# Graph-network kernel on one core: the layers of a tile one step closer to its edge sums, x loaded two steps ahead, the low parts of all tile sums on VectorE

## What is computed

```
h    = max(layernorm(x), 0)                              # 12500 x 128, eps 1e-5
agg  = segment_sum(edge_attr_48, dst, 12500)             # 12500 x 48
u    = graph_globals[0]                                  # one row for all nodes
out  = x + relu(concat(h, agg, u) @ W1 + b1) @ W2 + b2   # hidden width 256
```

## Time and profile before

| | us |
|---|---|
| median of 3 runs | 279.07 (278.94 to 281.57) |
| the profiled execution | 280.1 |
| its span, first to last instruction | 278.1 |
| TensorE busy in the span | 249.7 |
| VectorE busy | 218.8 |
| ScalarE busy | 145.0 |
| GpSimd busy | 103.1 |

### The profile page before, as it was taken

How to read it: one execution, slowest core, us unless ns; L and a number is a source line. 1 busy time by engine, 2 the same in 40 slices (tenths; PEclk the granted TensorE clock), 3 DMA queues, 4 the chain that set the end, 5 groups by cost and what they waited for, 6 DMA issues and landing times.

```text
span 278.1 us, 17414 instructions
## 1 busy us (share of the span) xinstructions
PE 249.7 (90%) x7448; PEld 200.0 (72%) x7448; DVE 218.8 (79%) x557; ACT 145.0 (52%) x315; POOL 103.1 (37%) x111
## 2 busy tenths in 40 slices
PE   7756468999999999989989989999899999999893
PEld 2646456887788779769768867877787787687572
DVE  1797737889988888968978888889789879885394
ACT  2555482564455556536544735654464455357640
POOL 9192103325532551451353245235415523532210
PEclk9977958999999999999999999999999999999998
DMA  7999958899999999999999999999999999999611
GB/s 250 368 364 341 336 182 273 271 387 365 388 384 384 386 378 388 366 380 345 379 359 370 388 380 338 390 379 386 380 366 382 378 357 387 369 333 380 257 40 57
DMA packets 70874, 94.50 MB, mean 340 GB/s; under 512 B 4324, under 2 KB 64260, under 8 KB 70854
## 3 DMA queue, kind: packets, MB, share of 16 engines
q1 hardware_dynamic: 69802, 94.29, 96.5%
q10 hardware_dynamic: 956, 0.00, 0.2%
q0 software_dynamic: 96, 0.00, 0.0%
HBM read 87.88 MB, written 6.40 MB: 339 GB/s over the span
## 4 chain that ended last, share of the span: by engine, by line
PE 62%; DMA 23%; DVE 7%; issue 3%; ACT 2%; POOL 1%; SPq 1%; DVEq 0%; POOLq 0%
PE group_bank L1051 22%; DMA edge_buf<-in_edge_attr 20%; PE hidden_bank L1098 12%; PE out_bank L1116 11%; PE window_bank L1073 6%; PE hidden_bank L1102 3%; PE hidden_bank L1104 3%; DMA x_buf<-in_x 3%; PE out_bank L1088 3%; DVE onehot L804 2%; PE window_bank L1138 2%; DVE rel_rows L759 2%; PE hidden_bank L1036 1%; ACT normed_x L601 1%; ACT rel L574 1%
## 5 line engine op out<-in xcount | busy, mean ns | idle before, releaser
L804 DVE TENSOR_TENSOR onehot<-rel,const_bank 128x896 f32<-128x896 f32 (+1 forms) x122 | 125.4, 1030 | 29.7 <-PE group_bank L1051 22.1
L1051 PE MATMUL group_bank<-edge_buf,onehot 128*32 128x48 f32 x6454 | 89.1, 211 | 6.4 <-DMA edge_buf<-in_edge_attr 3.6
L1051 PEld LDWEIGHTS group_bank<-edge_buf,onehot 128*32 128x32 f32 x6454 | 80.6, 113 | 15.5 <-DVE onehot L804 7.4
L535 POOL TENSOR_TENSOR tile_sums<-agg,tile_sums 48x512 fp32r<-48x512 f32 x22 | 28.1, 1277 | 133.1 <-ACT tile_sums L623 133.1
L1098 PE MATMUL hidden_bank<-normed_t,w_node 128*128 128x512 f32 (+1 forms) x100 | 52.7, 608 | 1.1 <-issue 1.0
L1116 PE MATMUL out_bank<-w_sb,hidden 128*128 128x128 f32 x384 | 47.7, 278 | 1.4 <-ACT normed_t L612 1.4
L1116 PEld LDWEIGHTS out_bank<-w_sb,hidden 128*128 128x128 f32 x384 | 44.7, 192 | 1.6 <-issue 1.6
L601 ACT ACTIVATE normed_x<-x_buf,shift,inverse 128x128 f32<-128x128 f32 x98 | 40.2, 482 | 1.9 <-DVE shift L864 1.9
L633 ACT ACTIVATE hidden<-hidden_bank,hidden_bias 128x512 f32<-128x512 f32 (+1 forms) x50 | 33.5, 671 | 13.3 <-PE hidden_bank L1104 13.3
L1102 PE MATMUL hidden_bank<-tile_sums,w_high 112*128 112x512 f32 (+1 forms) x50 | 39.3, 787 | 0.0
L586 ACT ACTIVATE sums_high<-group_bank 128x96 fp32r<-128x96 f32 (+1 forms) x49 | 13.2, 269 | 46.3 <-PE group_bank L1051 46.3
(11 more groups left out here) (93 smaller groups left out, 214.8 us busy)
## 6 DMA issues: line engine op xcount, KB each, us to landing
edge_buf<-in_edge_attr SPq DMA_DIRECT2D x97, 672.0 KB, 7.4
edge_buf<-in_edge_attr SPq DMA_DIRECT2D x24, 504.0 KB, 7.9
x_buf<-in_x SPq DMA_DIRECT2D x24, 256.0 KB, 8.6
out<-out_buf SPq DMA_DIRECT2D x23, 256.0 KB, 6.6
dst_rows<-in_dst SPq DMA_DIRECT2D x3, 448.5 KB, 8.7
dst_rows<-in_dst SPq DMA_DIRECT2D x1, 252.3 KB
out<-out_buf SPq DMA_DIRECT2D x1, 224.0 KB
edge_buf<-in_edge_attr SPq DMA_DIRECT2D x1, 168.0 KB, 6.7
```

The lines of the kernel that those rows point to most:

```text
L535: pool.tensor_tensor(sums_tile(k, STACK_LOW), agg_tile(k), sums_tile(k, 0).bitcast(fp32), ALU.subtract)\
L804: dve.tensor_tensor(onehot[:, c0:c0 + cols, :], rel[:, r0:r0 + cols].unsqueeze(2).to_broadcast([P, cols, WINDOW]), ramp_const.unsqueeze(1) ...
L1051: done = pe.matmul(group_bank[h][WINDOW * j:WINDOW * (j + 1), n * F_EDGE:(n + 1) * F_EDGE], onehot[:, (g0 + j) * EDGES_PER_ROW + r, :], ed ...
```

## The change

It reorders all five engines' lists.
- Layers: first_layer of tile s - 1 (not s - 2) runs in step s, after sums of part 1 and turn_x of tile s; second_layer of tile s - 2 follows the sums of part 0. Node matmuls of both halves come first, then the wait for tile_low.
- x of tile s + 2 is loaded in step s, after both parts of the edges; its moments are taken a step earlier.
- tile_low of every tile is VectorE's; GpSimd keeps x_plus_b2 and add_out. window_base is loaded at two places of a step, once each.
- dst blocks 1 to 3 are turned in steps 2 to 4. keep_clock runs 8 and 4 times, not 14 and 8. One of two GpSimd zeroings of agg goes ahead of places().
- In the tail the last tile of x is turned into `group_bank[1]`.

```diff
--- before.py
+++ after.py
@@ sync @@
-                if s < tiles - 1:
-                    load_x(last_tile() if s + 1 == tiles - 1 else At(s + 1))
+                    load_part(At(s + 1), 1)
+                if s + 2 < tiles:
+                    load_x(last_tile() if s + 2 == tiles - 1 else At(s + 2))
+                if s == 1:
+                    load_dst(3)
...
-                if s + 1 < steps:
-                    load_part(At(s + 1), 1)
@@ gpsimd @@
             for s in range(steps):
-                if 2 <= s < full_steps:
-                    pool.wait_ge(xb_ready, s)
-                    tile_low(At(s - 2))
-                    pool.wait_ge(tile_low_ready, s + 1)
-                if s >= 3:
-                    add_out(At(s - 3))
                 x_plus_b2(last_tile() if s == tiles - 1 else At(s))
-            add_out(At(tiles - 3))
+                if s >= 2:
+                    add_out(At(s - 2))
@@ scalar @@
+            for s in range(1, full_steps):
+                following = last_tile() if s + 1 == tiles - 1 else At(s + 1)
                 copy_sums(At(s), 0)
+                if s == 1:
+                    bias()
+                if s >= 2:
+                    copy_out(At(s - 2))
+                if 2 <= s <= blocks:
+                    copy_rel(s - 1)
+                tile_high(At(s - 1))
                 copy_sums(At(s), 1)
+                deviate(following)
+                relu_hidden(At(s - 1))
+                copy_turned(At(s))
+                normalise(following)
+                if s < blocks:
+                    relative(s)
@@ vector @@
             for s in range(1, full_steps):
                 n = At(s + 1)
+                add_window(At(s - 1), 1, base[1])
+                make_placing(At(s), 1)
...
                 make_onehot(n, 0)
+                base[0] = window_base(At(s), 0)
                 make_onehot(n, 1)
+                low_sums(At(s), 0)
                 make_onehot(n, 2)
+                add_window(At(s), 0, base[0])
+                make_placing(n, 0)
+                tile_low(At(s - 1))
                 make_onehot(n, 3)
+                low_sums(At(s), 1)
+                following = last_tile() if s + 1 == tiles - 1 else n
+                moments(following)
+                join_moments(following)
+                base[1] = window_base(At(s), 1)
                 make_onehot(n, 4)
+                invert(following)
@@ tensor @@
-            keep_clock(14, window_bank[0])
+            keep_clock(8, window_bank[0])
             turn_rel(0)
...
                 sum_part(step, 0)
+                with pe.If(i > blocks):
                     second_layer(step.plus(-2))
                 with pe.Else():
+                    with pe.If(i > 1):
+                        second_layer(step.plus(-2))
+                        turn_rel(i - 1)
...
+                place(step, 0)
+                sum_part(step, 1)
+                turn_x(step)
+                with pe.If(i > 0):
+                    pe.wait_ge(rel_ready, i * 2)
+                    first_layer(step.plus(-1))
+                place(step, 1)
```

More of the change, by code:

```diff
@@ L504, in _ @@
                 pool.memset(tile_sums[p][:, :].bitcast(fp32), 0.0).then_inc(stacks_zeroed, 1)
+            pool.memset(agg[:, 0, :], 0.0).then_inc(agg_zeroed, 1)
             places()
-            for j in (0, 1):
-                pool.memset(agg[:, j, :], 0.0).then_inc(agg_zeroed, 1)
+            pool.memset(agg[:, 1, :], 0.0).then_inc(agg_zeroed, 1)
             def x_plus_b2(k):
@@ L575, in copy_rel @@
                                    .rearrange("p (r g) -> p r g", g=P)[:, :, 0:rows], ACT.Copy)\
-                        .then_inc(rel_ready, 1)
+                        .then_inc(rel_ready, 2 * steps if (b, h) == (blocks - 1, 1) else 1)
             def copy_sums(s, h):
@@ L907, in _ @@
             make_placing(At(0), 1)
+            make_onehot(At(1), 1)
             invert(At(0))
-            make_onehot(At(1), 3)
             step_bases()
             base = [window_base(At(0), h) for h in range(2)]
+            make_onehot(At(1), 2)
+            low_sums(At(0), 1)
+            dve.wait_ge(agg_zeroed, 4)
+            add_window(At(0), 0, base[0])
+            make_placing(At(1), 0)
+            make_onehot(At(1), 3)
+            moments(At(1))
+            join_moments(At(1))
             make_onehot(At(1), 4)
-            dve.wait_ge(agg_zeroed, 4)
+            invert(At(1))
             for s in range(1, full_steps):
                 n = At(s + 1)
-                add_window(At(s - 1), 0, base[0])
-                low_sums(At(s - 1), 1)
+                add_window(At(s - 1), 1, base[1])
+                make_placing(At(s), 1)
+                if s == 1:
+                    dve.wait_ge(w1_high_ready, 1)
+                    dve.tensor_tensor(w1_low[:, :], w1_edge[:, :], w1_high[:, :].bitcast(fp32), ALU.subtract)\
+                       .then_inc(w1_split, 1)
                 if n.value * GROUPS % P + GROUPS > P:
@@ L920, in _ @@
                 make_onehot(n, 0)
-                if s == 2:
-                    dve.wait_ge(w1_high_ready, 1)
-                    dve.tensor_tensor(w1_low[:, :], w1_edge[:, :], w1_high[:, :].bitcast(fp32), ALU.subtract)\
-                       .then_inc(w1_split, 1)
-                moments(At(s))
+                base[0] = window_base(At(s), 0)
                 make_onehot(n, 1)
-                join_moments(At(s))
-                make_placing(At(s), 0)
+                low_sums(At(s), 0)
                 make_onehot(n, 2)
-                add_window(At(s - 1), 1, base[1])
-                low_sums(At(s), 0)
-                invert(At(s))
+                add_window(At(s), 0, base[0])
+                make_placing(n, 0)
+                tile_low(At(s - 1))
                 make_onehot(n, 3)
-                base = [window_base(At(s), h) for h in range(2)]
+                low_sums(At(s), 1)
[3 more added lines that the diff above has]
+                base[1] = window_base(At(s), 1)
                 make_onehot(n, 4)
-                make_placing(At(s), 1)
+                invert(following)
                 if s == 2 * blocks:
@@ L942, in _ @@
             second, last = At(tiles - 2), last_tile()
-            add_window(At(full_steps - 1), 0, base[0])
-            low_sums(At(full_steps - 1), 1)
-            moments(last)
-            make_placing(At(steps - 1), 0)
-            last_base = window_base(At(steps - 1), 0)
-            dve.wait_ge(tile_low_ready, tiles - 3 + 2)
-            tile_low(At(tiles - 3))
-            join_moments(last)
-            invert(last)
+            base[0] = window_base(At(steps - 1), 0)
             add_window(At(full_steps - 1), 1, base[1])
             low_sums(At(steps - 1), 0)
-            add_window(At(steps - 1), 0, last_base)
+            add_window(At(steps - 1), 0, base[0])
             tile_low(second)
@@ L1077, in place, with turn_x @@
                 done.then_inc(window_ready[h], 1)
-            def turn_x(k):
+            def turn_x(k, to_bank=turned_bank):
                 pe.wait_ge(normed, k.value + 1)
-                if isinstance(k, Again):
+                if to_bank is not turned_bank:
+                    pe.wait_ge(sums_split[1], full_steps + 1)
+                elif isinstance(k, Again):
                     pe.wait_ge(out_copied, k.value + 2)
@@ L1099, in first_layer @@
                               start=True, stop=False)
-                    if c == 0:
-                        pe.wait_ge(tile_low_ready, k.value + 3)
+                pe.wait_ge(tile_low_ready, k.value + 3)
+                for c in range(2):
                     pe.matmul(hidden_bank[c][:, 0:cols], w1_high[:, c * P:(c + 1) * P], tile_sums[own(k)][:, 0:cols],
@@ L1111, in second_layer @@
                     if not isinstance(k, Again):
-                        ahead = 3 if k.static and k.value == tiles - 3 else 2
-                        pe.wait_ge(turned_copied, k.plus(ahead).value + 1)
+                        pe.wait_ge(turned_copied, k.plus(2).value + 1)
                 for j in range(strips_of(k)):
@@ L1128, in sum_bias @@
                 pe.wait_ge(weights_in, 7 * 16)
-                pe.wait_ge(rel_ready, 4)
+                pe.wait_ge(rel_ready, 2)
                 for c in range(2):
```

92 lines of the change are left out of this document (22 added, 70 removed).

## The result

The changed kernel takes 291.54 us (median of 4 runs, 290.91 to 292.13), the kernel before 279.0 (278.42 to 281.57). The ratio is 1.043, with a 95% interval of 1.036 to 1.050. I had said 278.0, with a range of 269 to 285: it came out slower, and beyond the range. The profiled execution has a span of 290.2 us, where I had worked out 276.9.

A forecast was written before the change was run, and what follows sets the result against it. VectorE was to become the longest engine, 9.65 us a step plus a 0.5 wait, taken as 10.1. Start 36.9, three steps at 10.25, 18 at 10.1, then 14.15 and 13.3 gave span 276.9, median 278, range 269 to 285.

The forecast's parts named there:

- zero of step 2: End of the start: VectorE's first instruction of step 2 (add of part 1), forecast at 36.9 us.
- steps 2 to 4: The three steps with turn_rel and copy_rel, forecast at 10.25 us each.
- 18 steps: The steps after those with turn_rel up to step 23, forecast at 10.1 us each.
- zero of step 23 to the tests: The tail, from VectorE's add of part 1 in step 23 to the tests that end the kernel: 14.15 us.
- the tests to the end: The kernel's last stretch, forecast to stay at 13.3 us.
- w: Wait of VectorE's tile_low for GpSimd's x_plus_b2 in each step: 10.7 - P, 0.5 us, bounds 0 and 1.1.
- P: Period of a step, from VectorE's add of part 1 to the next: 9.65 + w, 10.17 us, taken as 10.1.
- the meeting: VectorE's tile_low waiting out a GpSimd add in progress, as both read SBUF; forecast wait 0.5 us a step.
- VectorE's loop without a meeting: VectorE's time per step: 8.5 + 0.61 (tile_low) + 0.27 (wait for tile_high) + 0.3 (register load) = 9.65 us.
- Rival 2: In most steps tile_low loses a whole GpSimd add: P of 10.55, about 287 us; chance 0.20.
- Rival 3: The start is not shortened, as the order waits on the transfers of ends_i: 282 us; chance 0.06.
- The placing table: In the start: table ready at 15.5 us, not 17.48, after which VectorE's list runs without pause.

The follow-up runs named there:

- run 2: Changed kernel, but ScalarE runs deviate of the next tile behind both relu_hidden, not ahead of them; 285.03 us, 1.019 of the kernel before.
- run 3: Changed kernel, but both register loads of window_base stand behind the first onehot of the step, as before the change; 275.82 us, 0.986 of before.
- run 1: Changed kernel, but GpSimd's x_plus_b2 of tile k also waits until tile_low of tile k - 2 is done; 274.88 us, 0.9845 of before.
- run 7: Changed kernel with x_plus_b2 waiting for tile_low, and ScalarE's relative moved right behind copy_sums of part 1; 273.82 us.
- run 4: Changed kernel, but TensorE's first test in the loop asks for step 0, so turn_places follows without a jump; 288.78 us.
- run 5: Changed kernel, but tile_low of tiles 0 to 22 is GpSimd's again, behind add_out of its step; 272.55 us, 0.975 of before.
- run 8: Changed kernel with x_plus_b2 waiting for tile_low, both register loads behind the first onehot, relative early and turn_places first among TensorE's branches; 273.45 us, 0.977 of before.
- run 9: Changed kernel with tile_low of tiles 0 to 22 on GpSimd, relative early and turn_places first among TensorE's branches; 272.3 us, 0.971 of before.
- run 10: Changed kernel with x_plus_b2 waiting for tile_low, and keep_clock again 14 and 8 times long; 275.65 us.
- run 11: Changed kernel with x_plus_b2 waiting for tile_low, relative early and turn_places first, without putting the register loads together; 274.14 us.
- Run 12: As run 8, but only a quarter of x is loaded for tiles 3 to 24, all other work unchanged; 270.49 us.

## Why the prediction was wrong

Its sum against the profile, stretch by stretch, with the borders that it used:

| | predicted | measured | off |
|---|---|---|---|
| zero of step 2 | 36.9 | 39.61 | +2.7 |
| steps 2 to 4 | 30.75 | 34.39 | +3.6 |
| 18 steps | 181.8 | 189.55 | +7.75 |
| zero of step 23 to the tests | 14.15 | 14.34 | +0.2 |
| the tests to the end | 13.3 | 12.3 | -1.0 |

**The step that failed is w.** "TensorE then needs 5.56, so the next sums start at 8.6 - P of the next step. Their 1.92 and the second layer's 1.99 bring copy_out to 12.55 - P." The first half is nearly right: the sums of part 0 begin at 166.56, which is 8.77 after the zero at 157.79. But second_layer does not follow them at once: it begins 0.51 behind their end, and copy_out at 171.12, 2.75 behind the next zero where 12.55 - P gives 1.97. It writes into out_bank, into which x was turned, so it waits for copy_turned; that stands on ScalarE behind relu_hidden, and that behind deviate, which waits for VectorE's mean_var. ScalarE idles 3.90 before deviate, the last 1.4 of it with the first hidden_bank ready to be copied. All of that was in the code; the start of second_layer was worked out from TensorE alone.

**With it falls the P in the formula.** I let the meeting shrink as steps got longer ("a longer loop moves copy_out forward, and w shrinks by as much"), because TensorE's part of the way did not contain w. The real way begins at mean_var, on VectorE, behind tile_low itself. From the end of mean_var x_plus_b2 is 6.29 us away, by ScalarE, TensorE and GpSimd, and tile_low 6.46, by VectorE. Both clocks start at the same event, so however long tile_low waits, in the next step the add is 0.17 ahead again, and w measures 0.95, not 0.5. In the prediction's terms: counted from the zero, x_plus_b2 begins at 14.6 - P by TensorE's way (12.55 - P, and 0.57, 0.07 and 1.41 behind it) or at 4.86 by the way from mean_var, whichever is later, and tile_low at 5.04. Behind step 5, with its P of 9.62, the add begins at 4.98, just as 14.6 - P says; from step 7 on, where 14.6 - P would be 4.0, it begins at 4.86 (in step 9 alone at 4.60). The prediction had the first way only. Run 2 cuts the second: second_layer then hangs on TensorE, and the formula holds with its own numbers (a mean P of 10.24 where 10.17 was worked out, w of 0.5, tile_low 1.17 where 1.2 was expected). Run 3 shows the tie from the other side: 0.3 us taken from VectorE's way only, and tile_low is first.

**What was right.** VectorE's loop without a meeting: 9.65, and run 1 has 9.61 to 9.65, so the prices of tile_low (0.61), the wait for tile_high (0.27) and the load (0.3) hold together; run 3's 9.3 gives 0.33 for the load alone. That a tile_low behind a GpSimd add waits it out: in steps 2 to 4 and in 17 of the 18. The tail up to the tests, to 0.2 us. Rival 2's price, 287 for an added 0.45 a step, was right for the 18 steps and lacked the start. Its chance of 0.20 was too low: I had called a lead of 0.1 us a race, and a w between its two ends hung on the P in the formula. Without that, only the ends are left. And the rivals were priced one at a time, but rivals 2 and 3 both came: 278, 9 for the one and 4 for the other make 291.

**Steps 2 to 4** were priced at 10.25 for TensorE's turning. They are 12.00, 11.15 and 11.24. The price of the turning itself was right: with no meeting and relative early (run 7) steps 3 and 4 are 10.34 and 10.52. Three things were missed. The first is turn_rel waiting for relative, which stands at the end of ScalarE's list: the three steps take 33.79 in run 1 and 32.43 in run 7. The second is the meeting, 0.6 (34.39 less 33.79). The third is that TensorE enters step 2 late. In run 7 step 2 is still 11.57, and the timeline shows why:

```profile
38.31 1.99 PE L1035 MATMUL group_bank<-edge_buf,onehot 128*32 128x48 f32 x168
38.52 0.37 DVE L817 TENSOR_TENSOR agg<-agg,window_bank 48x216 f32 x1 [0.53 <-PE window_bank L1057]
...
44.05 0.52 DVE L817 TENSOR_TENSOR agg<-agg,window_bank 48x352 f32 x1 [1.49 <-PE window_bank L1057]
...
48.65 1.99 PE L1035 MATMUL group_bank<-edge_buf,onehot 128*32 128x48 f32 x168
```

TensorE begins the sums of step 2 only 0.21 ahead of VectorE's zero (38.52), but those of step 3 1.44 ahead of the next (50.09). So place of part 0 is late in step 2 and VectorE waits 1.49 for it. That is the 1.2 between 11.57 and 10.34.

**The start.** "The placing table then is there at 15.5": it came at 17.22 + 0.29, 2.0 later, as at 17.48 before, by the branch of 3.44 us. Behind the table I had a list of 21.4 us. In run 4 the table is there at 15.05 and step 2 begins at 37.32, 22.3 later, of which 0.98 is VectorE waiting for TensorE's window. So the list was right, and the missed terms are the branch (2.0) and that wait (0.7 net). Rival 3 (a start not shortened) was right in its sign, turn_places later than 14 us, and had the wrong cause, the landing of ends_i. The slow clock of 18 to 33 us is no large part of it: run 2, granted 1.00 up to 23 us and 0.66 and 0.79 behind, begins step 2 at 39.40.

**The end.** From the tests on it takes 12.3, not 13.3. Those 13.3 had a meeting in them, too: in the kernel before, the third of the four tests on the order of dst began beside an add_out (timeline of before), and it took 2.04 where the others take 1.09. After the change the last add_out has ended by then.

```profile
266.85 1.34 POOL L530 TENSOR_TENSOR out_buf<-mlp_out,xb_buf 128x512 f32<-128x512 f32 x1 [7.43 <-ACT mlp_out L641]
...
267.09 2.04 DVE L759 CUSTOM_DVE_ANT_0 rel_rows<-dst_rows 128x896 f32<-128x896 int32 x1
```

**And the floor.** Eight kernels here have their 18 steps in 173.0 to 175.7 us (runs 1, 3, 5 and 7 to 11), and the kernel before in 174.2, at 372 to 379 GB/s where I had taken 385. What the good versions gain lies mostly ahead of step 5, which begins at 69.77 in run 5 and at 76.45 before. Run 12 puts the transfers' share at 3.6 us or more over the engines' own.

## What to carry to other kernels

Where two engines share something, don't ask only how long each holds it: trace the start of both back to a common event. If they hang on the same one, the order between them repeats in step after step, no lengthening of the loop loosens it, and a lead of 0.17 us cost 0.95 us each time here; then put an explicit wait where the loser has slack. And before an instruction is priced right behind its predecessor on its engine, look at every buffer it writes and at whose list frees that buffer.

## What the runs showed of the chip

- A branch of TensorE lasted 3.44 us in the changed kernel, where the same line's median is 0.17. The order of the cases in the code moves it: with that order the longest branch is 2.5 to 3.8 us in every run (1 to 3, 5, 7 and 10), with the order of run 4 it is 1.3 to 1.5 (4, 8, 9, 11 and 12), and the kernel before has none over 0.35. That it waits for code not yet loaded is my reading, and no run shows it. The Trainium skill, page "Advanced Engine Details and Errata", section "Control Flow Timing", gives about 108 ns for a compare-and-branch; the median here, 169 ns, is above that, and this one is far from both.
- TensorE paused for 3.5 us at 13 to 16 us in the changed kernel, and the granted clock was 1.2 GHz (0.50) from 18 to 33 us; without the pause it stayed at 2.4 (1.00) in run 4. That pair does not make the pause the cause. Runs 2 and 5 have the same pause (3.3 and 3.2 us) and 1.00 from 13 to 23 us, and runs 8 and 11, without it, have 0.84 from 18 to 23 and 0.66 to 28. What sets the clock in this stretch stays open.
- A tile_low that waits out an add ends 0.55 after that add's recorded end, and not 0.69: either 0.14 of its time lies ahead of the wait, or the add lets go 0.14 before its end. It is the same the other way round: in step 5 the add that waits ends 1.13 after tile_low, 0.14 less than its own 1.27.
